# Two biases of a graph network's layer added on POOL instead of by products, first norms in the set-up, and a new order

## The reference

```python
h_gat = relu(_layernorm(einsum('bmn,bnh->bmh', weighted_adj, h), gat_g, gat_b))
h_gin = (1.0 + eps) * h_gat + einsum('mn,bnh->bmh', A_final, h_gat)
z = einsum('bmh,hk->bmk', h_gin, W1) + b1
z = relu(_layernorm(z, mlp_g, mlp_b))
x_gin = einsum('bmk,ko->bmo', z, W2) + b2
return relu(x_gin + h_gat)
```

## Time and profile before

| | |
|---|---|
| Median of 3 runs | 1022.04 us |
| The three runs | 1020.98, 1022.04, 1031.19 us |
| Profiled execution | 1025.88 us |
| Its span | 1024.1 us |
| Mean granted PE clock | 0.974 of full |

### The profile page before, as it was taken

How to read it: one execution, slowest core, us unless ns; L and a number is a source line. 1 busy time by engine, 2 the same in 40 slices (tenths; PEclk the granted TensorE clock), 3 DMA queues, 4 the chain that set the end, 5 groups by cost and what they waited for, 6 DMA issues and landing times. The chain is left out here.

```text
span 1024.1 us, 21202 instructions
## 1 busy us (share of the span) xinstructions
PE 957.3 (93%) x7355; PEld 908.4 (89%) x7355; DVE 870.2 (85%) x2532; ACT 632.7 (62%) x1641; POOL 549.4 (54%) x1169
## 2 busy tenths in 40 slices
PE   6779999999999999999999999999999899997998
PEld 5679998998988899899989899999899899887897
DVE  5989797999989987978899889699989879779884
ACT  2446557686668653675575674777548584777741
POOL 3426254681786651755566464456727635467831
PEclk9878999999999998999999999999999999999999
DMA  7020000000020010002000101100000100000004
GB/s 141 2 62 2 1 2 1 2 2 1 2 83 2 2 42 2 1 21 63 2 1 1 43 1 42 43 2 22 22 1 2 42 2 2 1 1 2 1 1 124
DMA packets 38490, 20.17 MB, mean 20 GB/s; under 512 B 3184, under 2 KB 37872, under 8 KB 38384
## 3 DMA queue, kind: packets, MB, share of 16 engines
q1 hardware_dynamic: 36512, 18.42, 6.8%
q10 hardware_dynamic: 1872, 0.40, 0.2%
HBM read 10.43 MB, written 8.39 MB: 18 GB/s over the span
## 5 line engine op out<-in xcount | busy, mean ns | idle before, releaser
L639 PE MATMUL ps<-HE,PT 128*128 128x129 f32 x2048 | 241.0, 277 | 5.9 <-issue 2.3
L639 PEld LDWEIGHTS ps<-HE,PT 128*128 128x128 f32 x2048 | 234.8, 193 | 9.3 <-issue 8.6
L925 ACT ACTIVATE Y<-X,SM 128x128 f32<-128x128 f32 x512 | 203.9, 487 | 41.8 <-POOL SM L1083 41.7
L1068 POOL TENSOR_TENSOR SM<-ST 128x8 f32<-128x8 f32 x96 | 28.4, 296 | 294.9 <-DVE ST L1154 294.8
L1291 DVE SCALAR_TENSOR_TENSOR PT<-ps,CE,maskT 128x512 f32<-128x512 f32 x256 | 174.1, 742 | 13.7 <-PE ps L763 7.8
L1079 POOL TENSOR_TENSOR SM<-SM,minus_half 128x8 f32<-128x8 f32 x96 | 162.1, 1688 | 7.6
L639 PE MATMUL ps<-W,HT 128*128 128x128 f32 (+1 forms) x768 | 126.7, 312 | 0.7 <-issue 0.4
L639 PEld LDWEIGHTS ps<-W,HT 128*128 128x128 f32 x768 | 116.0, 193 | 10.1 <-ACT HT L918 0.6
L1154 DVE BATCH_NORM_STATS2 ST<-X 128x6 f32<-128x128 f32 x512 | 104.9, 277 | 3.2
L656 PE MATMUL ps<-ident,Y 128*128 128x128 f32 x640 | 86.5, 279 | 11.5 <-ACT Y L925 9.8
L656 PEld LDWEIGHTS ps<-ident,Y 128*128 128x128 f32 x640 | 72.5, 144 | 17.7 <-ACT Y L925 15.4
(11 more groups left out here) (262 smaller groups left out, 2348.9 us busy)
## 6 DMA issues: line engine op xcount, KB each, us to landing
X<-in_x_dram SPq DMA_DIRECT2D x32, 256.0 KB, 3.4
out_dram<-X SPq DMA_DIRECT2D x32, 256.0 KB, 2.8
adj_raw<-in_adj_dram SPq DMA_DIRECT2D x4, 256.0 KB, 3.7
W<-in_L_gnn_W_dram SPq DMA_DIRECT2D x1, 128.0 KB, 5.7
Ws<-n_L_gnn_self_weight_dram ACTq DMA_DIRECT2D x1, 64.0 KB, 3.1
W<-in_L_gnn_W_dram ACTq DMA_DIRECT2D x1, 64.0 KB, 3.5
feat2w<-in_L_gnn_W_dram ACTq DMA_DIRECT2D x1, 64.0 KB, 4.3
Wo<-L_gnn_others_weight_dram SPq DMA_DIRECT2D x1, 64.0 KB, 5.8
```

Source lines behind the costliest of these rows:

```text
L639: return nc.tensor.matmul(o, w, m, start=start, stop=stop, skip_group_check=True)
L925: a = A(dst[:, n, 0:F], src[:, n, 0:F], func, scale=SM[s][:, S_RSTD, n:n + 1], bias=SM[s][:, S_SHIFT, n:n + 1])
L1068: TT(sm[:, S_DIF, :], st[:, :, 1], st[:, :, 4], ALU.subtract)
```

## The change

Both biases leave PE. `bias_1` and `bias_2` (split, in rows 0 and 32 of tables for `pick`) are replaced by plain tiles `mlp_b1` and `mlp_b2` that hold the bias in every partition. POOL gets two new steps per group: `mlpz1` adds `mlp_b1` to `YF` after ACT's copy and before the stats, and `mlpv1` adds `mlp_b2` to `VA` in SBUF, at any time between `gatl1` and `mlpc1`. For this `VA` has to hold the ReLU, so ACT does a second ReLU operation in `gatl1`, in place, and DVE's operations in `gatl1` and `mlpc1` lose their maximum with zero.

The set-up takes over the stats, `rstd` and normalisation of groups 0 and 1 (`EARLY = 2`) and the 16 products of `erank` with their copies. The two sums over `maskT` on DVE are replaced by sums that ACT's copies of `maskT` give (eight copies of 128x256 with `accum_out` instead of two of 128x1024). The 16 narrow products of `strict` with `cnt_row` give way to four with `ident`. The loads are regrouped: ACT issues the weights first and then what the set-up needs of vectors, SP all three first groups ahead of the other parameters, and each user waits for its own part alone. `TURNS` and `HOMES` are new.

```diff
+EARLY = 2
 STEPS:
     ("gatl1", 0, "act dve"),
+    ("mlpv1", 0, "pool"),
     ("gin1", 2, "pe act"),
     ("mlpa1", 2, "pe act"),
+    ("mlpz1", 0, "pool"),
     ("mlps1", 0, "dve pool"),
 PREP:
-    ("erank", 4, "pe act"),
 TURNS:
-    "sp": ("403502611728394a5b6c7d8e9fdbceaf"),
+    "sp": ("2435061728394a5b6c7d8e9fbacdef"),
...
 set-up, POOL:
+                for s in range(EARLY):
+                    pool.wait_ge(sig["var"][s], 1)
+                    rstd_of(pool, link, s, False).then_inc(sig["rstd"][s], 1)
+                pool.wait_ge(loaded["rest"], 16 * len(REST))
+                nc.gpsimd.tensor_scalar(bias3[:], bias3[:], -1.0, None, ALU.add)
 set-up, PE:
+                for i in range(T):
+                    for j in range(T):
+                        mm = MM(ps[i // 2][:, (i % 2) * N:(i % 2 + 1) * N], maskT[:, j, i * P:(i + 1) * P],
+                                upper[:, j, :], start=(j == 0), stop=(j == T - 1))
+                    if i % 2 == 1:
+                        mm.then_inc(made["rank"], 1)
 set-up, ACT:
+                for s in range(EARLY):
+                    if s == 1:
+                        act.wait_ge(made["rowtot"], 1)
+                        A(rowtot_b[:], ps[3][:, 0:N], ACT.Copy)
+                        for h in range(2):
+                            act.wait_ge(made["rank"], h + 1)
+                            A(rank[:, 2 * h:2 * h + 2, :], ps[h][:].rearrange("p (a n) -> p a n", a=2), ACT.Copy)
+                    act.wait_ge(sig["rstd"][s], 1)
+                    scaled(Y[s], X[s], s, ACT.Relu).then_inc(sig["normed"][s], 1)
 set-up, DVE:
+                first_stats(0)
...
-                V.reduce_sum(cnt_low[:], mT[:, :, N // 2:N], AX_X)
-                link(V.reduce_sum(cnt_all[:], mT, AX_X))
+                link(V.tensor_tensor(cnt_all[:], cnt_half[:, :, 0], cnt_half[:, :, 1], ALU.add))
...
+                first_stats(1)
 PE, function mlp:
                     for h in range(2):
                         o, done = open_tile(u, name, s, h)
-                        MM(o, pick[:], repeat(bias[:], 2 * G), True, False)
                         for tt in range(2):
                             for b in range(G):
                                 c = (tt * G + b) * F
-                                mm = MM(o[:, c:c + F], blk(s, b, 2 * h + tt), w[:], False, True)
+                                mm = MM(o[:, c:c + F], blk(s, b, 2 * h + tt), w[:], True, True)
 ACT, function gatl1:
                     act.wait_ge(sig["gated"][s], count(u.g, 3, 0))
-                    A(HI[s][:], VA[s], ACT.Relu).then_inc(sig["hi"][s], 1)
+                    A(HI[s][:], VA[s], ACT.Relu)
+                    A(VA[s], VA[s], ACT.Relu).then_inc(sig["hi"][s], 1)
 POOL:
+                def mlpv1(u, s):
+                    pool.wait_ge(sig["lo"][s], count(u.g, len(LOS), LOS["1"]))
+                    TT(VA[s], VA[s], repeat(mlp_b2[:], TG), ALU.add).then_inc(sig["by_pool"][s], 1)
+
+                def mlpz1(u, s):
+                    for h in range(2):
+                        slot, k = u.tile("mlpa1", h)
+                        pool.wait_ge(taken[slot], k + 2)
+                    TT(YF[s], YF[s], repeat(mlp_b1[:], TG), ALU.add).then_inc(sig["by_pool"][s], 1)
 DVE:
                 def gatl1(u, s):
-                    V.scalar_tensor_tensor(out=LO[s], in0=VA[s], scalar=0.0, in1=HI[s][:].bitcast(F32),
-                                           op0=ALU.max, op1=ALU.subtract).then_inc(sig["lo"][s], 1)
+                    V.tensor_tensor(LO[s], VA[s], HI[s][:].bitcast(F32), ALU.subtract).then_inc(sig["lo"][s], 1)
                 def mlps1(u, s):
-                    for h in range(2):
-                        read_by_act(u, "mlpa1", s, h)
+                    dve.wait_ge(sig["by_pool"][s], count(u.g, 6, 3))
                     stats(u, s, lambda n: Y[s][:, n, 0:F])
                 def mlpc1(u, s):
-                        V.scalar_tensor_tensor(out=YF[s][:, r, :], in0=VA[s][:, r, :], scalar=0.0,
-                                               in1=o.rearrange("p (r f) -> p r f", f=F), op0=ALU.max,
-                                               op1=ALU.add).then_inc(read, 1)
+                        V.tensor_tensor(YF[s][:, r, :], VA[s][:, r, :], o.rearrange("p (r f) -> p r f", f=F),
+                                        ALU.add).then_inc(read, 1)
```

More of the change, by code:

```diff
@@ L427, in gnn_kernel, with scaled @@
+        def scaled(dst, src, s, func):
+            for n in range(TG):
+                a = nc.scalar.activation(dst[:, n, 0:F], src[:, n, 0:F], func, scale=SM[s][:, S_RSTD, n:n + 1],
+                                         bias=SM[s][:, S_SHIFT, n:n + 1])
+            return a
         with nc.Block() as block:
@@ L431, in _ @@
                     sp.dma_start(adj_raw[:, t, :], adj[t * P:(t + 1) * P, :]).then_inc(adj_loaded, 16)
-                for s in range(1):
+                for s in range(NS // 2):
                     for b in range(G):
@@ L675, in coefb0 @@
                 def coefb0(u, s):
[L677 removed]
+                    pe.wait_ge(sig["by_pool"][s], count(u.g, 6, 0))
                     o, done = open_tile(u, "coefb0", s)
@@ L798, in gin1, with mlp @@
                         mm.then_inc(done, 1)
-                def mlp(u, name, s, w, bias, before):
+                def mlp(u, name, s, w, before):
                     for b in range(G):
@@ L808, in mlp @@
                                 c = (tt * G + b) * F
-                                mm = MM(o[:, c:c + F], blk(s, b, 2 * h + tt), w[:], False, True)
-                        mm.then_inc(done, 1)
-                def erank(u, s):
-                    for i in range(T):
-                        o, done = open_tile(u, "erank", s, i)
-                        for j in range(T):
-                            mm = MM(o, maskT[:, j, i * P:(i + 1) * P], upper[:, j, :], j == 0, j == T - 1)
+                                mm = MM(o[:, c:c + F], blk(s, b, 2 * h + tt), w[:], True, True)
                         mm.then_inc(done, 1)
@@ L828, in eedge @@
                 def eedge(u, s):
-                    for i in range(T):
-                        turned(u, "erank", s, i)
                     for t, src in enumerate((adjn, rank)):
@@ L894, in _ @@
                     "att2b": lambda u, s: attend(u, "att2b", s, 1),
-                    "mlpa1": lambda u, s: mlp(u, "mlpa1", s, W1, bias_1, "gin1"),
-                    "mlpc1": lambda u, s: mlp(u, "mlpc1", s, W2, bias_2, "mlpb1"),
+                    "mlpa1": lambda u, s: mlp(u, "mlpa1", s, W1, "gin1"),
+                    "mlpc1": lambda u, s: mlp(u, "mlpc1", s, W2, "mlpb1"),
                 }
@@ L923, in normalise @@
                     act.wait_ge(sig["rstd"][s], count(u.g, NLN, ln_at[name]))
[L924 to L927 removed]
+                    scaled(dst, src, s, func).then_inc(sig["normed"][s], 1)
                 def cmax0(u, s):
@@ L999, in feat3 @@
                         A(HI[s][:, t * G:(t + 1) * G, :], v[:, :, F:2 * F], ACT.Copy).then_inc(sig["hi"][s], 1)
-                def erank(u, s):
-                    for i in range(T):
-                        o, read = filled(u, "erank", s, i)
-                        A(rank[:, i, :], o, ACT.Copy).then_inc(read, 1)
                 def eedge(u, s):
```

350 lines of the change are left out of this document (178 added, 172 removed).

## The result

| kernel | runs | median | lowest to highest |
|---|---|---|---|
| before | 4 | 1022.58 us | 1020.98 to 1031.19 |
| changed | 4 | 1038.09 us | 1031.11 to 1044.60 |
| changed, a second time beside before (1022.73) | 6 | 1046.25 us | 1033.99 to 1048.61 |

The ratio to before is 1.0144 with a 95% interval of 1.0094 to 1.0195, and 1.0211 (1.0172 to 1.0251) the second time. 1005.2 us and "faster" were forecast; the change makes the kernel 1.4 to 2.1% slower. The profiled execution took 1043.08 us.

A forecast was written before the change was run, and what follows sets the result against it. PE was taken to set the pace through the middle, DVE the set-up and first steps. Terms -19.8 - 5 + 0 + 4 + 3 + 1 = -16.8 us from the median 1022.04 gave 1005.2 us, range 994 to 1017.

The forecast's parts named there:

- The new places of the other steps I count at nothing.: Order of all engines' steps: groups' steps stand close to where they were, so no cost was counted.
- Bias products -19.8 us: PE: dropping the 64 products of pick and bias frees 0.31 us each, 19.8 us in all.
- the floor of zero: Bias products on PE: if the others don't wait for PE, freed time turns idle and the gain is zero.
- 0.17 at half the loss: First rival: half of PE's freed 19.8 us stays unused and the chain costs 8, giving 1015 us; chance 0.17.
- The new link +4: mlpz1 on POOL between ACT's copy and DVE's stats, 2.4 us per group: 4 us more, bounds 0 and 38.
- the port +3: POOL and DVE at the same memory: 32 additions hold up DVE by 10 us, 3 reaching PE, between 0 and 10.
- The bound of 38 us: Upper bound of the new link's cost: all 16 groups show the full 2.4 us of mlpz1.
- the second rival: Slower: the chain carries the pace, all 16 groups show mlpz1's 2.4 us, +38 us, giving 1035 us; chance 0.07.
- the +3 and +1 of the other terms: POOL and DVE at the same memory, +3 us; second ReLU on ACT in gatl1, +1 us.
- Ranks and first norms -5 us: Set-up: erank's products and two groups' first norms move into PE's idle time, gaining 5 us, between 3.2 and 6.3.
- the two marks given: PE's busy share in the middle: 95% or more for the forecast, 93% or below for the first rival.
- wrong altogether: Signs: the seam comes after 33 us, or PE's waits for ACT's normalisation more than double.

The follow-up runs named there:

- setup_only: Changed kernel's set-up with the old order and biases by products (high part only), against the kernel before: 1022.10 us, ratio 1.0009.
- a_products: setup_only with the new order (TURNS and HOMES) in place of the old, biases still by products: 1049.32 us, ratio 1.0256.
- a_noadd: Changed kernel without the two POOL additions; signals, second ReLU and new order stay: 1030.71 us, ratio 1.0087.
- b_noprod: Kernel before without the 64 products of bias and pick, nothing in their place, old order: 1025.27 us, ratio 1.0014.
- b_pooladd: Kernel before with both bias additions on POOL right ahead of mlps1, second ReLU on ACT, old order: 1095.99 us, ratio 1.0705.
- b_late: b_pooladd with the stats of YF one or two steps later on DVE in 13 of 16 groups, other engines unchanged: 1105.18 us.
- the halves: a_products with the old order for the first half: 1031.63 us; setup_only with the new order for the first half: 1038.04 us.
- warm: setup_only with products nobody reads filling PE's idle time at the start: 1020.96 us, ratio 0.9992.
- a_warm: Changed kernel with 22 turns of ident that nobody reads at the end of PE's set-up: 1045.28 us.
- b_both: b_noprod with DVE's addition to X in the second layer cut to one of eight blocks: 1015.88 us, ratio 0.9924.

## Why the prediction was wrong

The parts as measured: the set-up -1.0 us (setup_only against before), the order +27.2 (a_products against setup_only), the products -18.6 (a_noadd against a_products), the additions +13.1. From 1023.1 that makes 1043.8. Each part is uncertain by 3 to 6 us, and the parts hold along this path alone, since they depend on each other. In the old order the products are worth nothing (b_noprod) and the additions with the second ReLU cost 71 us (b_pooladd against b_noprod), where the changed kernel ends 52 us below b_pooladd. So the new order costs 27 us without the additions and, against the one placement of them that was tried in the old order, is worth some 50 with them.

- *"The new places of the other steps I count at nothing."* This is the step that failed: the term is +27 us where nothing else of the chain is changed. It was judged by how near a step stands to its old place, but over half of PE's, ACT's and DVE's steps stand elsewhere. In a fixed order a move of one or two places can decide which engine stands in front of a semaphore (b_late shows it), and the halves (+16, +9.5) show that the loss adds up over the program.
- *Bias products -19.8 us.* 0.31 us apiece came out in the new order (-18.6, the second ReLU included), though PE idles more there; in the old order it is 0 (b_noprod). Part of the 18.6 goes along with the clock (0.957 in a_products' profile, 0.965 in a_noadd's), so that it lies near the 19.8 is no proof of the term. The text had named the floor of zero; the chance that it got, 0.17 at half the loss, was too small, because a busy share of 96% was read as "PE sets the pace".
- *The new link +4, the port +3.* Together with the second ReLU 8 us were forecast; without the ReLU, which a_noadd keeps, 7, and 13 were measured in the new order (7 by the first four runs). Which of the two terms is the larger one wasn't tried there. POOL's total (624.0 us for 625) and the additions' length (2.2 us for 2.4) came near the forecast, and so did what POOL does to DVE: summed over DVE's lines, the lengths beyond the lines' medians are 34.2 us for 21.4 before (some 30 expected) and 20.4 in a_noadd, so that 32 additions cost DVE 14 us, 0.4 us apiece. The rule that the prediction took from the Trainium skill, page "SBUF — State Buffer", section "Who interferes with whom", would by the prediction's estimate have given 77 us more on DVE if each addition held it for its whole length; that isn't seen.
- *The chain in the old order.* The bound of 38 us was too low for the place that b_pooladd gives the additions: 49 us for the link alone, 71 with the other addition ahead of it (both with the second ReLU). Slack was counted on the chain copy to normalisation, on ACT and PE. The engine that paid was DVE, whose stats follow the link directly and whose queue holds other groups' work. So the second rival's mechanism exists in the old order, at a higher price than it named, and the new order trades it for its own loss. Its time, 1035 us (which leaves out the +3 and +1 of the other terms), is near the result for another reason, by luck; its sign, over 40 us of idle time ahead of ACT's `Y<-Y,SM`, reads 9.8.
- *Ranks and first norms -5 us.* The seam moved from 29.85 to about 28 us and the first turn to 28.12, both as forecast or better. Yet setup_only gains 1 us by the medians and nothing by the ratio (1.0009), less than a measurement tells: what left PE was followed by 12.27 us of waiting for DVE's `row_of`. The question "what is late next" had been asked of the seam, not of the edge part behind it.
- *What would show it.* PE's busy time fell by 10 us, not 30. The 30.9 us of the bias products overlap the products beside them, which the prediction says itself: without them b_noprod is busy for only 16.2 us less at nearly the same clock (0.970 for 0.974). The rest goes along with the lower clock, at which products are longer. The middle's share, 94.1%, lies between the two marks given. Neither sign of "wrong altogether" appeared (seam by 28 us; PE's wait for the normalisation 12.1 for 9.8 us), although the forecast was wrong: they watched the new parts, and nothing watched the order.

## What to carry to other kernels

A high busy share does not show that an engine sets the pace where every engine follows a fixed order: here an engine at 96% could lose 20 us of work and the time stayed. Before giving a price to freed time, look behind each freed piece for the wait that ends later. Where a change rewrites the order of the work, that is a term of its own, to be priced or at least bounded; a kernel with the new order and little else of the change, and hybrids that switch orders where both have done the same steps, measure it in a few runs. Expect such a term to depend on the rest: this order lost 27 us without the additions for which it makes room. When a link is put into a chain, follow it along every engine's queue: b_late shows the wait moving to the next engine whose step comes too early.

## What the runs showed of the hardware

A short wait of PE can be followed by a stretch at the lower clock. The changed kernel, around 221, 296 and 729 us, and then around 430 and 490 us (columns as in the stretches above):

```profile
220.00:223.00 3.00, 1.13 (x10) 0.89 (x9) 2.97 (x9) 0.67 (x4) 2.84 (x4) 0.94 0.00 0
223.00:226.40 3.40, 3.40 (x19) 3.40 (x18) 3.30 (x9) 3.40 (x14) 3.03 (x9) 0.55 0.02 5
226.40:232.00 5.60, 5.59 (x50) 5.40 (x50) 5.13 (x14) 2.86 (x8) 4.68 (x5) 1.00 0.00 0
...
295.00:298.00 3.00, 1.15 (x6) 0.74 (x5) 1.94 (x3) 3.00 (x9) 2.48 (x7) 0.95 0.41 116
298.00:301.40 3.40, 3.40 (x12) 2.78 (x12) 1.75 (x3) 2.80 (x7) 3.07 (x5) 0.54 0.46 130
301.40:307.00 5.60, 5.60 (x44) 5.23 (x43) 3.92 (x15) 2.33 (x5) 5.39 (x9) 1.00 0.15 46
...
727.30:731.00 3.70, 0.46 (x5) 0.41 (x4) 3.66 (x7) 1.52 (x8) 2.12 (x1) 1.00 0.49 143
731.00:734.40 3.40, 3.36 (x17) 3.17 (x15) 3.27 (x7) 3.04 (x10) 0.00 (x0) 0.53 0.16 46
...
429.00:431.50 2.50, 0.02 (x1) 0.00 (x0) 2.50 (x11) 1.63 (x4) 1.05 (x1) 1.00 0.00 0
431.50:434.90 3.40, 3.35 (x29) 3.35 (x30) 2.88 (x18) 0.00 (x1) 2.78 (x11) 1.00 0.00 0
...
485.00:492.30 7.30, 7.22 (x62) 6.83 (x61) 4.95 (x21) 4.02 (x13) 2.93 (x12) 1.00 0.51 144
492.30:495.70 3.40, 2.52 (x12) 2.52 (x13) 2.45 (x15) 0.78 (x5) 2.41 (x6) 0.50 0.02 5
```

In the first three places PE idles for 1.9 to 3.2 us and then works at 0.53 to 0.55, near the level of 1.2 GHz; behind the first two the rows show it back at 2.4. Such a wait of 1.9 us costs another 1.5 us (an estimate: 3.4 us at 0.55 give as much as 1.9 us at full clock). It is no rule that a wait alone decides: a wait of 2.5 us at 429 us is followed by the full clock, and at 492 us the lower level comes behind 7.3 us in which PE was busy for 7.22. Over the whole span the mean clock fell from 0.974 to 0.959: 0.015 x 1041 = 16 us of PE's full speed, an estimate. Warm shows that speed given back at one place need not reach the end.

The runs of the changed kernel are ordered by that clock, those of the kernel before only roughly. The changed kernel took 1031.1 to 1034.0 us in the three runs at 0.972 to 0.975, 1040.8 to 1043.1 in the two at 0.959 to 0.964 and 1044.6 to 1048.6 in the five at 0.953 to 0.955. The kernel before, in its eleven runs at 0.972 to 0.975, took 1020.3 to 1028.5, with a median of 1021.6. So some 10 to 12 of the 21 us remain at an equal clock and the rest goes along with a lower one. Whether the lower clock causes the longer time or the waits cause both isn't settled: a_warm ran at 0.953 to 0.966 like the changed kernel, and nothing that was tried raised the clock of the whole span without changing the waits.

No version that does all the work beat the kernel before by more than a measurement tells; warm came nearest, at 0.9992. b_both, at 0.9924, leaves out both biases and most of an addition.
